# One root and one set of scales for two row vectors: pairing x and h of a unit in a fused scan and feed-forward kernel

## The reference, cut to what matters

```
xc   = silu(conv(ctx @ w_in) + b);  B, C, dt from xc
state[n] = state[n] * exp(dt * A[n]) + dt * xc * B[n]       # 16 states, scanned over 512 steps
y    = (sum_n state[n] * C[n] + D * xc) * silu(layernorm(x))
x    = x + tanh(g_x) * y
v    = layernorm(x)
xq   = quantize(rmsnorm(v));  h = silu(xq @ Wg) * (xq @ Wu)  # ternary weights, F = 2048
hq   = quantize(rmsnorm(h));  x = x + tanh(g_f) * (hq @ Wd)
rmsnorm(r)  = r * rsqrt(mean(r*r) + 1e-6)
quantize(r) = round(r * s) / s,  s = 127 / max(|r|, 1e-5)    # one s for each row
```

## Time and profile before

| | us |
|---|---|
| median of 3 runs | 612.67 (612.07 to 612.9) |
| the profiled execution's own time | 611.89 |
| span of its trace | 609.9 |
| DVE busy | 556.6 (91%), 766 instructions |
| POOL busy | 521.0 (85%), 298 instructions |
| PE busy | 516.7 (85%) |
| ACT busy | 507.7 (83%), 776 instructions |

### The profile page before, as it was taken

The page is one execution under the profiler, slowest core; times in us unless marked ns, Lnnn a source line. Parts: engine busy times, 40 slices in busy tenths (PEclk is TensorE's granted clock), DMA queues, the critical chain, the costliest instruction groups (busy, mean ns, idle before and its releaser), DMA issues. The chain is left out here.

```text
span 609.9 us, 9603 instructions
## 1 busy us (share of the span) xinstructions
PE 516.7 (85%) x3190; PEld 359.8 (59%) x3190; DVE 556.6 (91%) x766; ACT 507.7 (83%) x776; POOL 521.0 (85%) x298
## 2 busy tenths in 40 slices
PE   6999676768675888989879898989789999998997
PEld 2443265747564676767656767675667575764443
DVE  1899989999999899999899999998999999988774
ACT  3879788986999789899978898998798989777773
POOL 1558799999999899999999899999998999973340
PEclk9999859778799999999999999999999999999999
DMA  8992951530661010115521111145411110000323
GB/s 273 403 412 108 325 197 34 192 136 1 240 243 53 0 53 2 35 34 208 203 93 35 34 37 36 35 157 223 121 35 35 36 36 18 1 18 21 84 53 86
DMA packets 38866, 66.32 MB, mean 109 GB/s; under 512 B 12177, under 2 KB 20369, under 8 KB 36002
## 3 DMA queue, kind: packets, MB, share of 16 engines
q1 hardware_dynamic: 38818, 65.72, 30.9%
HBM read 55.49 MB, written 8.13 MB: 104 GB/s over the span
## 5 line engine op out<-in xcount | busy, mean ns | idle before, releaser
L889 POOL TENSOR_TENSOR area_s<-area_s,b_bc 128x1024 f32<-128x1024 f32 x117 | 275.2, 2364 | 14.1 <-DVE u_all L1510 9.9
L515 PE MATMUL pY<-ident,area_s 128*128 128x128 f32 x532 | 87.9, 291 | 54.5 <-DVE area_s L1518 54.5
L584 PE MATMUL pG<-wq_gu,area_f 128*128 128x512 fp8e4 x448 | 108.0, 380 | 4.2 <-ACT area_f L1106 2.9
L1510 DVE TENSOR_TENSOR_SCAN area_s<-pA,area_s 128x512 f32<-128x512 f32 x88 | 105.1, 1205 | 5.1 <-ACT pA L1169 5.1
L515 PEld LDWEIGHTS pY<-ident,area_s 128*128 128x128 f32 x532 | 62.2, 146 | 75.4 <-DVE area_s L1518 67.9
L1169 ACT ACTIVATE pA<-dt_all,a_neg 128x512 f32<-128x512 f32 x145 | 97.7, 682 | 10.7 <-DVE area_s L1510 5.9
L881 POOL TENSOR_TENSOR u_all<-u_all 128x1024 f32<-128x1024 f32 x44 | 103.9, 2361 | 0.2 <-DMA u_all<-bc_rows 0.2
L1518 DVE TENSOR_TENSOR area_s<-area_s,pC 128x512 f32<-128x512 f32 x132 | 87.0, 661 | 0.9 <-DVE area_s L1510 0.8
L509 PE MATMUL pC<-ident,xdT 128*128 128x128 f32 x528 | 84.2, 288 | 3.2 <-DVE area_s L1518 2.0
L584 PEld LDWEIGHTS pG<-wq_gu,area_f 128*128 128x128 bf16 x448 | 41.6, 98 | 48.9 <-ACT area_f L1106 5.2
L509 PEld LDWEIGHTS pC<-ident,xdT 128*128 128x128 f32 x528 | 65.4, 146 | 8.1 <-DVE area_s L1518 6.6
(11 more groups left out here) (218 smaller groups left out, 1123.0 us busy)
## 6 DMA issues: line engine op xcount, KB each, us to landing
b_bc<-bc_rows SPq DMA_DIRECT2D x14, 1024.0 KB, 6.7
area_s<-x SPq DMA_DIRECT2D x32, 256.0 KB, 2.9
u_all<-bc_rows SPq DMA_DIRECT2D x14, 512.0 KB, 6.5
b_bc<-w_gate SPq DMA_DIRECT2D x1, 4096.0 KB, 14.0
dt_all<-x SPq DMA_DIRECT2D x1, 4096.0 KB, 24.3
area_f<-w_up SPq DMA_DIRECT2D x1, 4096.0 KB, 33.6
area_f<-w_down SPq DMA_DIRECT2D x1, 4096.0 KB, 14.9
out<-area_f SPq DMA_DIRECT2D x16, 256.0 KB, 2.1
```

Of the source, the lines that this page charges most:

```text
L515: mm = pe.matmul(pY[:, k * P:(k + 1) * P], src[:, k * P:(k + 1) * P], ident[:, :], is_transpose=True, start=(first and k == 0), stop=(last ...
L584: mm = pe.matmul(bank, xqT[t % 2][:, k, :], wq_gu[:, k, m, c * GW:(c + 1) * GW], start=(k == 0), stop=(k == NT - 1))
L889: gp.tensor_tensor(db[c % NDB], du[s % 2].rearrange("p (a l) -> p a l", a=1).to_broadcast([P, CH, L]), b_bc[:, CH * c:CH * c + CH, :], ALU ...
L1510: dve.tensor_tensor_scan(h, at, dbu, 0.0, ALU.mult, ALU.add).then_inc(S["s_scan"], 1)
```

## The change

Call a tile t2 joint if it is not the last of its batch and t2 + 1 is under 12. For a joint t2, unit s = t2 + 5 has x of tile t1 = t2 + 1 and h of tile t2 at hand; POOL then forms both roots by one power on two adjacent columns (`both_rstd`, in the place of `h_rstd`), and DVE forms both sets of scales by five instructions on two adjacent columns (`both_scales`, in the place of `h_scales`). The maximum over x is taken in the tile's own unit after scan 1 (`x_max`), no longer in the unit before. The columns are numbered anew so that the pairs lie side by side. On ACT `scale_x` moves from step 2 to step 5 and `copy_xqT` from step 4 to step 6, for every t1 that is not a multiple of 4; on PE the transposes of x move behind the down products and one pooled sum, and into pG[1], with the second part of h waiting for the copy. The factor of x changes its sign, and the copy changes it back.

```diff
@@ -98,11 +98,19 @@
-VE, RR, M2, REC1, XS, SS, RH, M3, REC2, FAC, MH, XSUM, DEV = range(13)
+VE, SS, RR, RH, M2, MH, MX, M3, REC1, REC2, XS, FAC, XSUM, DEV = range(14)
 PSS, PMH, SPARE = 20, 24, 28
-CS, EC, OSC = (14, 15), (16, 17), (18, 19)
+CS, OSC, EC = (14, 16), (17, 15), (18, 19)
 ROOT_F = F ** 0.5
+
+
+def joint(t):
+
+    return t % NT != NT - 1 and t + 1 < UNITS - NT
+
+
+SOLO_AT = [sum(not joint(i) for i in range(t)) for t in range(UNITS + 1)]
 def osc(t):
...
@@ -283,6 +292,21 @@
             return sm[:, i:i + 1]
+
+        def pair(i):
+            return sm[:, i:i + 2]
+
+        def wait_h_root(eng, t):
+            if joint(t):
+                eng.wait_ge(S["f_rr"], t + 2)
+            else:
+                eng.wait_ge(S["f_rh"], SOLO_AT[t] + 1)
+
+        def wait_h_scale(eng, t, which):
+            if joint(t):
+                eng.wait_ge(S["f_xs"], 5 * t + 6 + which)
+            else:
+                eng.wait_ge(S["f_hs"], 4 * SOLO_AT[t] + which)
         @block.sync
@@ -696,17 +720,17 @@
                     c_bcast(s, 3)
-                if t1 % NT:
-                    pe.wait_ge(S["f_h"], FC * t1)
-                    xq_transpose(t1, pG[0])
                 fill(s, early, 4)
                 y_sum_pooled(s, 0)
+                if t1 % NT:
+                    pe.wait_ge(S["f_h"], FC * t1)
+                    xq_transpose(t1, pG[1])
                 if t2 >= 0:
+                    hq_transpose(t2, 0, pG)
                     if t1 % NT:
                         pe.wait_ge(S["f_xqT"], t1 + 1)
-                    hq_transpose(t2, 0, pG)
                     hq_transpose(t2, 1, pG)
@@ -825,6 +849,8 @@
             gp.memset(neg_half[:, :], -0.5).then_inc(S["k_const"], 1)
+            gp.memset(eps_pair[:, 0:1], Q_EPS).then_inc(S["f_j"], 1)
+            gp.memset(eps_pair[:, 1:2], Q_EPS / ROOT_F).then_inc(S["f_j"], 1)
             gp.wait_ge(S["k_const"], 9)
@@ -866,8 +892,18 @@
                 gp.wait_ge(S["f_sq"], 2 * t + (2 if t < UNITS - 1 else 1))
-                past(gp, S["f_hs"], 4 * t)
+                if t:
+                    wait_h_scale(gp, t - 1, 4)
                 gp.tensor_tensor(col(RH), col(SS), neg_half[:, 0:1], ALU.pow).then_inc(S["f_rh"], 1)
+
+            def both_rstd(t):
+
+                gp.wait_ge(S["f_ve"], t + 2)
+                gp.wait_ge(S["f_sq"], 2 * t + 2)
+                past(gp, S["f_xs"], 5 * (t + 1))
+                if t:
+                    wait_h_scale(gp, t - 1, 4)
+                gp.tensor_tensor(pair(RR), pair(VE), neg_half[:, 0:2], ALU.pow).then_inc(S["f_rr"], 1)
             def dt_u(s):
@@ -925,7 +961,10 @@
                 if t2 >= 0:
-                    h_rstd(t2)
+                    if joint(t2):
+                        both_rstd(t2)
+                    else:
+                        h_rstd(t2)
                 residual(s - 1)
@@ -933,15 +972,11 @@
                 times_b(s, NDB + 2)
-                if t1 % NT and (t1 + 1) % NT:
-                    x_rstd(t1 + 1)
                 times_c(s, 1)
                     times_b(s + 1, 0)
-                if t1 % NT == 0:
-                    x_rstd(t1 + 1)
                 times_c(s, 2)
...
@@ -1103,7 +1138,7 @@
                 past(act, S["f_up"], FC * (t - 1))
-                act.activation(xqT[t % 2], bank.rearrange("p (k t) -> p k t", t=P), ACT.Copy, bias=-MAGIC).then_inc(S["f_xqT"], 1)
+                act.activation(xqT[t % 2], bank.rearrange("p (k t) -> p k t", t=P), ACT.Copy, scale=-1.0, bias=MAGIC).then_inc(S["f_xqT"], 1)
             def gate_silu(t, c, bank):
...
@@ -1246,7 +1282,7 @@
                         w_sign(2, 0)
-                    if n == (2 if t1 % NT else 7):
+                    if n == (5 if t1 % NT else 7):
                         scale_x(t1)
@@ -1261,10 +1297,10 @@
                         centre(t1)
-                    if n == (4 if t1 % NT else 9):
-                        copy_xqT(t1, pG[0][:, :])
                     if n in (5, 6) and t2 >= 0:
                         scale_h(t2, n - 5)
+                    if n == (6 if t1 % NT else 9):
+                        copy_xqT(t1, pG[1 if t1 % NT else 0][:, :])
                     if n == 7 and t1 % NT == 0:
...
@@ -1438,20 +1474,40 @@
                 dve.tensor_scalar(col(VE), mv[:, 1:2], 1.0 + RMS_EPS, RMS_EPS * LN_EPS, ALU.mult, ALU.add).then_inc(S["f_ve"], 1)
+            def x_max(t):
+
+                dve.wait_ge(S["f_xn"], t + (2 if t % NT == 0 and t < UNITS - NT else 1))
+                dve.tensor_reduce(col(M2), xn[t % 2], AX, ALU.max, apply_absolute_value=True).then_inc(S["f_xs"], 1)
+
             def x_scales(t):
-                m2 = col(M2)
-
-                dve.wait_ge(S["f_xn"], t + (2 if t % NT == 0 and t < UNITS - NT else 1))
-                dve.tensor_reduce(m2, xn[t % 2], AX, ALU.max, apply_absolute_value=True).then_inc(S["f_xs"], 1)
+                x_max(t)
                 dve.wait_ge(S["f_xs"], 5 * t + 1)
                 dve.wait_ge(S["f_rr"], t + 1)
-                dve.tensor_scalar(m2, m2, col(RR), Q_EPS, ALU.mult, ALU.max).then_inc(S["f_xs"], 1)
+                dve.tensor_scalar(col(MX), col(M2), col(RR), Q_EPS, ALU.mult, ALU.max).then_inc(S["f_xs"], 1)
                 dve.wait_ge(S["f_xs"], 5 * t + 2)
                 past(dve, S["f_e"], t)
-                dve.reciprocal(col(REC1), m2).then_inc(S["f_xs"], 1)
+                dve.reciprocal(col(REC1), col(MX)).then_inc(S["f_xs"], 1)
                 dve.wait_ge(S["f_xs"], 5 * t + 3)
-                dve.tensor_scalar(col(XS), col(REC1), -127.0, col(RR), ALU.mult, ALU.mult).then_inc(S["f_xs"], 1)
-                dve.tensor_scalar(col(CS[t % 2]), m2, k_gate[:, :], None, ALU.mult).then_inc(S["f_xs"], 1)
+                dve.tensor_scalar(col(XS), col(REC1), 127.0, col(RR), ALU.mult, ALU.mult).then_inc(S["f_xs"], 1)
+                dve.tensor_scalar(col(CS[t % 2]), col(MX), k_gate, None, ALU.mult).then_inc(S["f_xs"], 1)
+
+            def both_scales(t):
+
+                x = t + 1
+                dve.wait_ge(S["f_xs"], 5 * x + 1)
+                dve.wait_ge(S["f_mh"], t + 1)
+                dve.wait_ge(S["f_rr"], x + 1)
+                i = 2 + t + 1 - SOLO_AT[t]
+                dve.tensor_tensor(pair(MX), pair(M2), pair(RR), ALU.mult).then_inc(S["f_j"], 1)
+                dve.wait_ge(S["f_j"], i)
+                dve.tensor_tensor(pair(MX), pair(MX), eps_pair[:, :], ALU.max).then_inc(S["f_xs"], 1)
+                dve.wait_ge(S["f_xs"], 5 * x + 2)
+                dve.wait_ge(S["f_e"], x)
+                dve.reciprocal(pair(REC1), pair(MX)).then_inc(S["f_xs"], 1)
+                dve.wait_ge(S["f_xs"], 5 * x + 3)
+                dve.scalar_tensor_tensor(out=pair(XS), in0=pair(REC1), scalar=127.0, in1=pair(RR),
+                                         op0=ALU.mult, op1=ALU.mult).then_inc(S["f_xs"], 1)
+                dve.tensor_tensor(pair(CS[x % 2]), pair(MX), k_pair[:, :], ALU.mult).then_inc(S["f_xs"], 1)
             def times_up(t, c, bank):
@@ -1469,18 +1525,18 @@
             def h_scales(t):
-                dve.wait_ge(S["f_rh"], t + 1)
+                wait_h_root(dve, t)
                 dve.wait_ge(S["f_mh"], t + 1)
                 dve.tensor_scalar(col(M3), col(MH), col(RH), Q_EPS / ROOT_F, ALU.mult, ALU.max).then_inc(S["f_hs"], 1)
-                dve.wait_ge(S["f_hs"], 4 * t + 1)
+                dve.wait_ge(S["f_hs"], 4 * SOLO_AT[t] + 1)
                 dve.reciprocal(col(REC2), col(M3)).then_inc(S["f_hs"], 1)
-                dve.wait_ge(S["f_hs"], 4 * t + 2)
+                dve.wait_ge(S["f_hs"], 4 * SOLO_AT[t] + 2)
                 past(dve, S["f_hp"], t - DMA_FROM)
                 dve.tensor_scalar(col(FAC), col(REC2), 127.0, col(RH), ALU.mult, ALU.mult).then_inc(S["f_hs"], 1)
-                dve.tensor_scalar(col(osc(t)), col(M3), k_out[:, :], None, ALU.mult).then_inc(S["f_hs"], 1)
+                dve.tensor_scalar(col(osc(t)), col(M3), k_out, None, ALU.mult).then_inc(S["f_hs"], 1)
             def output(t):
-                dve.wait_ge(S["f_hs"], 4 * t + 4)
+                wait_h_scale(dve, t, 4)
                 dve.wait_ge(S["f_dn"], t + 1)
@@ -1551,14 +1607,17 @@
                         h_max(t2)
+                    if n == 1 and t1 % NT:
+                        x_max(t1)
                     if n == 4 and t2 >= 0:
-                        h_scales(t2)
+                        if joint(t2):
+                            both_scales(t2)
+                        else:
+                            h_scales(t2)
                     if n == 4 and t1 % NT == 0:
                         x_scales(t1)
-                    if n == (11 if t1 % NT else 13) and (t1 + 1) % NT:
-                        x_scales(t1 + 1)
                     if n in (13, 14, 15):
...
```

(22 more changed lines are left out.)

## The result

| | before | changed |
|---|---|---|
| median of 4 runs, us | 612.72 (612.07 to 612.9) | 648.0 (647.52 to 649.05) |
| span of the trace, us | 609.9 | 647.0 |
| DVE busy, us | 556.6 (91%) | 563.0 (87%) |
| POOL busy, us | 521.0 (85%) | 518.5 (80%) |
| mean granted clock of PE | 0.966 | 0.945 |

The ratio is 1.0588 (95% interval 1.0574 to 1.0603). By the medians the changed kernel is 35.3 us slower, where 15.1 were forecast and 633.5 was the upper end. The direction was right, the size more than twice too small.

A forecast was written before the change was run, and what follows sets the result against it. The prediction took a relay of DVE (scan 14 to FAC) and ACT (FAC to scan 14) as the bound. Nine joint units at 0.76 + 0.92 = 1.68 us add 15.1 us to 612.67, giving 627.8 us; range 617 to 633.5.

The forecast's parts named there:

- What bounds the kernel: Middle-stage unit: a relay, 15.42 us of DVE from scan 14 to FAC, then 14.92 us led by ACT to scan 14.
- What is removed: x_scales on DVE in nine units and one POOL power of 0.58 us in nine: gain 0, at most 4.2 us.
- DVE's half: Scan 14 to FAC: x_max 0.60 us plus one more instruction 0.16, together 0.76 us a unit, bounds 0.55 and 1.16.
- ACT's half: FAC to scan 14: scale_x and copy_xqT add 1.28 us, 0.36 absorbed, net 0.92 us a unit, bounds 0.6 and 1.28.
- The handover of PE: PE's transposes after copy_xqT: the third part of h just arrives when ACT needs it, cost 0.
- rival with late transposes: ACT waits for PE's transposes at step 6 or 7 or 8: 0.5 us a unit, 4.5 more, 632.3; chance 0.14.
- The sum: Nine joint units: each grows by 0.76 + 0.92 = 1.68 us, 15.1 us in all, 627.8 on the median.

The follow-up runs named there:

- narrow maximum: Kernel before, with the maximum over x taken over 1 of its 512 columns in nine tiles: 611.77 us, ratio 0.9991.
- single columns: Changed kernel, every both_scales instruction with two SBUF tensors made into two one-column tensor_scalar instructions (seven instead of five): 628.7 us, ratio 1.028.
- one more maximum: Kernel before, with an unused maximum over 512 columns added on DVE after scan 1 of the nine units: 617.78 us, ratio 1.0096.
- the probe: Kernel before, with a one-column tensor_scalar and a tensor_tensor on the same columns added on DVE after scan 11, units 5 to 15: 618.29 us, one execution.
- the first experiment: Changed kernel, only the first two two-column instructions of both_scales (product, maximum) made into two one-column tensor_scalar instructions: 639.9 us, ratio to before 1.045.

## Why the prediction was wrong

- *What bounds the kernel.* Right in kind: a relay of DVE and ACT, with slack after scan 11. The equal periods of units 6 and 7 gave it, and the narrow maximum bore it out. The place of the hand-over was wrong, scan 10 and not FAC. In the changed kernel this cost nothing, since ACT's queue decided there. In single columns, where the clock held, exponential 13 of unit 6 starts 8.38 us after FAC, 0.83 us after scan 10 has ended; in the kernel before scan 10 ended 7.43 us after FAC and exponential 13 followed at once. The difference, 0.95 us, is what the half grew by.
- *What is removed: 0.* Right.
- *DVE's half: 0.76 us.* This is the first step that failed. The upper bound of a two-column form with two tensors was set by "292 ns for a 128-column tensor sum", whatever POOL was doing beside it. That sum does have both tensors in SBUF, but POOL was idle over it:

```profile
551.20 0.29 DVE L1576 TENSOR_TENSOR dt_all<-szT,area_s 128x128 f32<-128x128 f32 x1
```

```profile
552.77 0.55 POOL L864 TENSOR_TENSOR sm<-sm,neg_half 128x1 f32<-128x1 f32 x1 [7.82 <-DVE sm L1439]
```

  The wait is 1.25 - 0.16 = 1.09 us, nine times 9.8 us. Without it the half grew by 1.78 - 1.09 = 0.69, of which the maximum is 0.60, as forecast and as measured with one more maximum; 0.09 are left for the one instruction more, where 0.16 was taken. The wait's condition, a running POOL, was named nowhere in the forecast, which quoted the rule on op count and not the one told at the probe. The upper bound of 1.16 us a unit lay below the 1.78. Before, no DVE instruction of the middle stage with two tensors had both in SBUF: each took one from PSUM.
- *ACT's half: 0.92 us.* Right where the clock held (0.93 and 0.95).
- *The handover of PE: 0.* The second step that failed. It was timed at the durations of a full clock, and the waits for the copy were seen but not asked about the clock. In seven of nine units the clock fell to 0.50, the four transposes took 1.12 us for 0.66 and the four products 1.91 for 1.03. It cost 12.0 us. The rival with late transposes had its place right, and a mechanism and a price (4.5 us) that were wrong.
- *The sum.* 6.2 (DVE) + 8.4 (ACT) = 14.6, where 15.1 was forecast; with 9.8 for the wait on POOL and 12.0 for the clock that makes 36.4. With the wait removed and most of the clock back, single columns ran at 628.7, by the forecast's 627.8.

What stays open: why the clock falls in units 6 and 7 and not in 5 and 9 with the same three waits, and why it fell in one unit of single columns and in six of the first experiment with nearly the same two. The runs show what the low clock costs and that work in PE's gaps prevents it; they don't give a rule for when it comes. No run shows either whether POOL waits when DVE starts first.

## What to carry to other kernels

Count inputs by where they lie. A DVE instruction of two columns with both tensors in SBUF can cost as much as the POOL instruction beside it; the same work with a column scalar costs 0.21 us, so seven such instructions beat five. When an edit makes PE wait, look at the granted clock after the wait, and price what follows at both levels. And before an instruction is moved, ask which half of the relay it leaves and which it enters, and where one engine hands over to the other.

## What the runs showed of the hardware that was not expected

- A small DVE instruction with two SBUF tensors that started beside a POOL instruction ended within some 0.02 us of POOL's, in 29 of 29 cases (nine in the changed kernel, nine in the first experiment, eleven in the probe; 0.35 to 1.44 us long); with a column scalar in place of the second tensor it took 0.20 to 0.21 us in eleven of eleven. POOL's instructions weren't longer for it (2.36 us). One that began 0.06 us or so before POOL's end, right behind the factors' instruction in the first experiment, took its usual 0.15 us.
- Two-column instructions with POOL idle took 0.15 to 0.17 us, less than the 0.21 of one column with a column scalar.
- In seven of nine units the granted clock went to 0.50 during the last of three waits of some 0.6, 0.51 and 1.48 us, for 3.4 us (6.8 in two); eight small transposes in the first two kept it at 1.00 in all nine.
